# Attention and feed-forward layer: v loads behind the shift rows, the loop over sequences written out, constants filled as words, and another order of the copies of v

## What is computed

```python
xn  = layernorm(x)                                   # eps 1e-5
q, k, v = heads(xn @ Wq.T), heads(xn @ Wk.T), heads(xn @ Wv.T)
attend  = (abs(i - j) <= 128) | (i < 1) | (j < 1)    # a band, and token 0 to and from all
w   = softmax(where(attend, q @ k.T / sqrt(16), -inf))
x   = x + (w @ v) @ Wo.T
xn  = layernorm(x)
h   = bitlinear(xn, w_fc) + gate * (xn @ v2.T @ fast_b.T @ u.T)
out = x + bitlinear(relu(h) ** 2, w_proj)            # ternary weights with a scale
```

## Time and profile before

| | |
|---|---|
| median of 3 executions | 1406.53 us (1406.45 to 1410.13) |
| the profiled execution | 1413.2 us, span of its instructions 1410.8 us |
| mean granted TensorE clock | 0.936 of full speed |
| busy, of the span | PE 1223.1 us (87%), DVE 986.7 (70%), ACT 792.5 (56%), POOL 727.9 (52%) |
| DMA | 145.4 MB, queue of SP 37.8% of 16 engines' span |

### The profile page before, as it was taken

One profiled execution on the slowest core, in us unless ns is written; L12 is line 12 of the kernel. 1 busy time (PEld: TensorE's weight loads), 2 busy tenths in 40 slices (PEclk: granted clock), 3 DMA queues, 4 the chain that ended last, 5 costly groups with the idle time before them and its releaser, 6 DMA issues. The chain is left out here.

```text
span 1410.8 us, 31634 instructions
## 1 busy us (share of the span) xinstructions
PE 1223.1 (87%) x9122; PEld 807.0 (57%) x9122; DVE 986.7 (70%) x3217; ACT 792.5 (56%) x1315; POOL 727.9 (52%) x934
## 2 busy tenths in 40 slices
PE   4888885489998989889998998974699999999997
PEld 3777772044444444444444444433588888888886
DVE  5777762478787878678787787826477767777674
ACT  3555562067676767667676776762344545445454
POOL 1444443957676756667576675770143433433343
PEclk9999997589999999999999999995799999999999
DMA  2566754754246442455326543211311212122100
GB/s 86 194 221 221 234 193 117 124 119 110 69 105 150 115 118 72 107 119 133 97 79 136 120 105 99 60 56 45 120 46 46 90 45 89 45 61 72 45 31 30
DMA packets 141282, 145.43 MB, mean 103 GB/s; under 512 B 23085, under 2 KB 134721, under 8 KB 141121
## 3 DMA queue, kind: packets, MB, share of 16 engines
q1 hardware_dynamic: 141120, 143.55, 37.8%
HBM read 91.74 MB, written 50.95 MB: 101 GB/s over the span
## 5 line engine op out<-in xcount | busy, mean ns | idle before, releaser
L1124 DVE CUSTOM_DVE_ANT_0 a_masked<-a_turn,a_band 128x387 f32<-128x387 f32 (+1 forms) x1024 | 506.4, 537 | 128.4 <-PE a_turn L997 100.1
L1078 ACT ACTIVATE a_weights<-a_score 128x1024 f32<-128x1024 f32 x384 | 385.3, 1021 | 116.8 <-PE a_score L1017 116.3
L997 PE MATMUL a_turn<-a_k,a_q 96*128 96x387 bf16 (+1 forms) x1024 | 335.8, 339 | 23.2 <-DMA a_q<-q_parts 12.2
L1017 PE MATMUL a_score<-a_q,a_k 128*128 128x384 bf16 (+2 forms) x1408 | 282.3, 286 | 48.2 <-DMA a_q<-a_shift 47.8
L1381 POOL TENSOR_TENSOR f_square<-f_relu 128x512 f32<-128x512 f32 x128 | 150.5, 1179 | 296.4 <-ACT f_relu L1477 295.4
L894 POOL TENSOR_SCALAR_AFFINE_SELECT a_weights<-a_weights 128x1024 f32<-128x1024 f32 x256 | 275.8, 1090 | 53.2 <-ACT a_weights L1078 53.2
L997 PEld LDWEIGHTS a_turn<-a_k,a_q 96*128 96x128 bf16 x1024 | 96.8, 98 | 215.7 <-DVE a_max L1124 118.0
L1039 PE MATMUL a_sum<-a_weights,a_v 128*17 128x384 f32 (+2 forms) x2816 | 212.7, 400 | 2.3 <-POOL a_weights L894 2.2
L1017 PEld LDWEIGHTS a_score<-a_q,a_k 128*128 128x128 bf16 x1408 | 139.8, 101 | 110.5 <-issue 53.6
L1477 ACT ACTIVATE f_relu<-f_bank 128x512 f32<-128x512 f32 x128 | 76.5, 598 | 187.9 <-PE f_bank L207 184.7
L1509 DVE TENSOR_TENSOR f_square_lo<-f_square,f_square_hi 128x512 fp32r<-128x512 f32 x128 | 108.2, 856 | 88.8 <-POOL f_square L1381 88.8
(11 more groups left out here) (194 smaller groups left out, 2048.9 us busy)
## 6 DMA issues: line engine op xcount, KB each, us to landing
k_parts<-p_k_parts SPq DMA_DIRECT2D x96, 129.0 KB, 2.7
a_k<-k_parts SPq DMA_DIRECT2D x64, 193.5 KB, 3.7
a_k<-k_parts SPq DMA_DIRECT2D x192, 64.5 KB, 3.2
q_parts<-p_q_parts SPq DMA_DIRECT2D x96, 128.0 KB, 2.7
a_q<-q_parts SPq DMA_DIRECT2D x64, 192.0 KB, 3.3
a_q<-q_parts SPq DMA_DIRECT2D x192, 64.0 KB, 3.0
v_ones<-p_va SPq DMA_DIRECT2D x16, 544.0 KB, 3.4
p_x<-in_x SPq DMA_DIRECT2D x16, 512.0 KB, 5.1
```

The costliest lines, as they stand in the source:

```text
L997: pe.matmul(turn[TURN_OF_TILE[j] % TURN_BANKS][:, lo:hi], qw[ux.gpar][ux.hq][0:SLOT_ROWS, h, t * P:t * P + P], kt[ux.hq][0:SLOT_ROWS, h, s ...
L1017: ins = pe.matmul(score[c % 2][:, (n % 2) * GT + col * P:(n % 2) * GT + (col + m) * P], kt[us.hq][:, h, k0:k0 + P], qw[us.gpar][us.hq][:, ...
L1078: act.activation(pe_w[:, us.upar, c * CHUNK:(c + 1) * CHUNK], score[c % 2][:], ACT.Exp).then_inc(s_exp, 1)
L1124: dve.tensor_tensor_reduce(out=masked[:, ux.upar, h, t:t + hi - lo], in0=bank[:, lo:hi], in1=band[:, lo:hi], scale=1.0, scalar=NEG, op0=AL ...
```

## The change

- Projection: ACT makes the copies of v of the first two products ahead of the fourth middle part (`mid(2 * KT - 1)`) instead of behind it.
- `march`: the loop over sequences is a Python loop; all 64 units are written out, with constants in place of registers.
- SP in the attention: the load of v moves from `L_MAX` to `L_SHIFT`, one step later, and with `v0` behind the three shift rows of its step. The rows wait for a new semaphore of the zero fills (`s_zero`) in the first 8 units.
- The fills are made over fp32 words (a bitcast; one word of two bf16 ones for k), half the elements. POOL fills the eight q tiles first and then the k tiles 2 and 3; DVE fills the k tiles 0 and 1 ahead of its first unit. PE waits for each k tile by a semaphore of its own.
- The register waits (`Turn`) of POOL (`exp_turn`) and DVE (`tile_turn`) in the attention become waits for constants.

```diff
--- before.py
+++ after.py
@@ -47,6 +47,8 @@
 QSCALE = 1.0 / float(np.sqrt(HD))
 NEG = -3.0e38
 ROUND = 4
+
+TWO_ONES = float(np.array([0x3F803F80], np.uint32).view(np.float32)[0])
 DMA = 16
 
 
@@ -507,10 +509,11 @@
                     if u == 2 and (t := at(LN)):
                         norm.root(act, t)
                 if q:
-                    mid(2 * KT - 1)
                     if isinstance(q.g, int) and q.g == 0:
                         act.wait_ge(s_ones, 1)
                     for t in range(TB):
+                        if t == 2:
+                            mid(2 * KT - 1)
                         act.wait_ge(s_v, q.g * TB + t + 1)
                         act.activation(va[:, bass.ds(q.g * TB + t, 1), :].rearrange("p a (h e) -> p (a h) e", e=VW)
                                        [:, :, 0:HD],
@@ -651,9 +654,7 @@
             return Unit(b - 1, j + UPB)
         return at
 
-    for i in range(UPB):
-        body(step(0, i))
-    with eng.Fori(1, B) as b:
+    for b in range(B):
         for i in range(UPB):
             body(step(b, i))
     for i in range(lags):
@@ -771,7 +772,8 @@
         sum_bank = ctx.enter_context(nc.psum_tensor("a_sum", [P, GT], F32))
         turn = [ctx.enter_context(nc.psum_tensor(f"a_turn{i}", [P, GT], F32)) for i in range(TURN_BANKS)]
 
-        s_init, s_pool, s_ones = sem("init"), sem("pool_init"), sem("ones")
+        s_init, s_pool, s_zero = sem("init"), sem("pool_init"), sem("zero")
+        s_ones = [sem(f"ones{q}") for q in range(UPG)]
         s_load = [[sem(f"qk_in{g}{q}") for q in range(UPG)] for g in range(2)]
         s_v, s_v0 = [sem("v_in0"), sem("v_in1")], [sem(f"v0_in{q}") for q in range(UPG)]
         s_row = [sem("row0"), sem("row1")]
@@ -825,7 +827,16 @@
                         for n, part in enumerate(SINGLES[which]):
                             sp.dma_start(dst[(PARTS + n) * HD:(PARTS + n + 1) * HD], src[:, PLACE[which][part]]
                                          ).then_inc(landed, DMA)
-                if (u := at(L_MAX)) and u.hq == 0:
+                if u := at(L_SHIFT):
+                    if isinstance(u.n, int) and u.n < 2 * UPG:
+                        sp.wait_ge(s_zero, 2 * u.hq + 2)
+                    for part, ready in ((HIGH, s_high), (MID, s_mid), (LOW, s_low)):
+                        sp.wait_ge(ready, u.n + 1)
+                        row = qw[u.gpar][u.hq][SLOT_ROWS + part:SLOT_ROWS + part + 1, :, :]
+                        sp.dma_start(row.rearrange("s h (t q) -> s (h t) q", q=P),
+                                     shift[:, u.upar, part, :]).then_inc(s_row[u.upar], DMA)
+
+                if (u := at(L_SHIFT)) and u.hq == 0:
 
                     wait(sp, s_sum, (u.n - UPG * 2) + UPG)
                     lo, hi = window(u.gi)
@@ -838,15 +849,6 @@
                     cols = slice(u.hq * NQ * VW, (u.hq + 1) * NQ * VW)
                     sp.dma_start(v0[:, cols], va_dram[bass.ds(u.batch * T, 1), cols].to_broadcast((P, NQ * VW))
                                  ).then_inc(s_v0[u.hq], DMA)
-                if u := at(L_SHIFT):
-                    if isinstance(u.n, int) and u.n < 2 * UPG:
-                        sp.wait_ge(s_ones, u.hq + 1)
-                    for part, ready in ((HIGH, s_high), (MID, s_mid), (LOW, s_low)):
-                        sp.wait_ge(ready, u.n + 1)
-                        row = qw[u.gpar][u.hq][SLOT_ROWS + part:SLOT_ROWS + part + 1, :, :]
-                        sp.dma_start(row.rearrange("s h (t q) -> s (h t) q", q=P),
-                                     shift[:, u.upar, part, :]).then_inc(s_row[u.upar], DMA)
-
                 if (u := at(L_SHIFT)) and isinstance(u.n, int) and u.n == UNITS - 1:
                     ahead.load_weights(sp)
                 if (u := at(L_OUT)) and u.hq == UPG - 1:
@@ -879,16 +881,18 @@
                                pattern=[[0, NQ], [P, TB]], channel_multiplier=1).then_inc(s_pool, 1)
             pool.wait_ge(s_pool, 6)
             for q in range(UPG):
-                pool.memset(qw[0][q][SLOT_ROWS:P], 0.0)
-                pool.memset(qw[1][q][SLOT_ROWS:P], 0.0)
-                pool.memset(kt[q][SLOT_ROWS:P], 1.0).then_inc(s_ones, 1)
-                pool.wait_ge(s_ones, q + 1)
-            exp_turn = Turn(pool, s_exp, "exp_turn", CHUNKS // 2, CHUNKS // 2)
+                for g in range(2):
+                    pool.memset(qw[g][q][SLOT_ROWS:P].bitcast(F32), 0.0).then_inc(s_zero, 1)
+            for q in range(UPG // 2, UPG):
+                pool.memset(kt[q][SLOT_ROWS:P].bitcast(F32), TWO_ONES).then_inc(s_ones[q], 1)
+            pool.wait_ge(s_zero, 2 * UPG)
+            for q in range(UPG // 2, UPG):
+                pool.wait_ge(s_ones[q], 1)
 
             def cut(u, half, side):
 
                 if side == 0:
-                    exp_turn.wait(u.n * CHUNKS + (half + 1) * CHUNKS // 2)
+                    pool.wait_ge(s_exp, u.n * CHUNKS + (half + 1) * CHUNKS // 2)
                 first, sign = ((CUT_AHEAD, 1), (CUT_BEHIND, -1))[side]
                 blocks = pe_w[:, u.upar].rearrange("p (a c q) -> p a c q", a=2, q=P)[:, half, first::CUT_STEP, :]
                 pool.affine_select(out=blocks, in_=blocks, compare_op=ALU.is_ge, fill=0.0, base=0,
@@ -1006,7 +1010,7 @@
                     c = n // 2
                     if n == 0:
                         if isinstance(us.n, int) and us.n < UPG:
-                            pe.wait_ge(s_ones, us.n + 1)
+                            pe.wait_ge(s_ones[us.hq], 1)
                         pe.wait_ge(s_row[us.upar], (us.uhalf + 1) * DMA * SHIFT_ROWS)
                     if n % 2 == 0:
                         wait(pe, s_exp, us.n * CHUNKS + c - 1)
@@ -1101,8 +1105,9 @@
             dve.memset(score[1][:], 0.0).then_inc(s_init, 1)
             dve.memset(sum_bank[:], 0.0).then_inc(s_init, 1)
             dve.wait_ge(s_pool, 4)
+            for q in range(UPG // 2):
+                dve.memset(kt[q][SLOT_ROWS:P].bitcast(F32), TWO_ONES).then_inc(s_ones[q], 1)
             dve.wait_ge(s_pool, 6)
-            tile_turn = Turn(dve, s_tile, "tile_turn", 1)
 
             def body(at):
                 ux, um, uo = at(L_MAX), at(L_SHIFT), at(L_OUT)
@@ -1119,7 +1124,7 @@
                         bank, c = turn[TURN_OF_TILE[j] % TURN_BANKS], h * TB + t
                         if j == 0:
                             wait(dve, s_d0, ux.n - 1)
-                        tile_turn.wait(ux.n * TILES + j + 1)
+                        dve.wait_ge(s_tile, ux.n * TILES + j + 1)
 
                         dve.tensor_tensor_reduce(
                             out=masked[:, ux.upar, h, t:t + hi - lo], in0=bank[:, lo:hi],
```

## The result

| | before | after |
|---|---|---|
| median of the runs | 1406.49 us (1400.85 to 1410.13, 4 runs) | 1315.84 us (1313.05 to 1321.77, 4 runs) |
| the profiled execution | 1413.2 us, span 1410.8 | 1313.8 us, span 1312.1 |
| mean granted TensorE clock | 0.936 | 0.964 |

The changed kernel takes 0.936 of the time before (95% interval 0.932 to 0.941). The forecast was 1319 us, 1297 to 1347, and "faster" with 0.95: it held. The saving between the two profiled executions is 99 us where the sum of the forecast was 87. So the total came out, and the question is whether the parts did.

What follows compares the result with a forecast made beforehand. PE was taken as the bound, with its idle waits as the target. Savings of 20 + 16 + 33 + 13 + 5 = 87 us from the median of 1406.5 gave 1319 us, range 1297 to 1347.

Steps and rivals of the forecast that it cites:

- What bounds it: PE, busy 87% of the span, idles for the shift rows (47.8 us) and the projection's copies of v (24.3 us).
- Copies of v: Projection: two copies ahead of ACT's fourth middle part shorten PE's wait in each group; 20 us, ends 8 and 26.
- Fills: Attention's start: word fills by POOL and DVE let the first shift rows land sooner; 16 us, ends 14 and 18.
- rival D: Attention's start: fills cost by byte, so word fills are no shorter; 1322 us, chance 0.03.
- v behind the small transfers: Attention: without v ahead the shift rows land sooner, in ten waits of PE; 33 us, ends 15 and 43.
- Loop: Attention: writing the loop out removes the stop of all engines at two backward branches; 13 us, ends 9 and 14.
- Rival C: Attention: straight-line code can't be fetched as fast as five engines use it; slower, 1425 us, chance 0.03.
- Register waits: Attention: constant waits wake DVE sooner for a unit's first tile, 0.08 us in 60 units; 5 us, ends 0 and 15.
- A: Attention: rows stay late behind k, q and in four places the 127-row store; half of 33 us lost, 1336, chance 0.13.
- B: Projection: the gain is only 8 us because DVE or SP becomes its bound; 1331 us, chance 0.10.
- E: More comes free: PE's full clock earlier at the attention's start or no slow stretches in the projection; 1290, chance 0.06.

Runs made afterwards that it cites:

- n_act_dma: The changed kernel, but in the projection ACT instead of SP issues the store of v and the loads of x from the fifth group on; 0.924, 1304.0 us.
- a_fills_back: The changed kernel with the fills as before: bf16 elements, all twelve on POOL, in the old order; 0.947 of the time before, 1334.7 us.
- a_pool_only: The changed kernel, but POOL makes all the word fills and DVE none; 0.937 of the time before, 1318.3 us.
- n_store_late: The changed kernel, but SP waits for a finished group and stores it one step later, behind that step's loads and rows; 0.932, 1311.6 us.
- a_loop_back: The changed kernel with the loop over the last three sequences and the register waits of DVE and POOL back; 0.950, 1338.8 us.
- a_v_back: The changed kernel with the load of v again one step earlier and, like v0, ahead of the shift rows; 0.966, 1360.6 us.
- b_v_move: The kernel before with one edit alone: the load of v one step later and behind the shift rows, v0 behind it; 0.976, 1375.9 us.
- a_v_split: The changed kernel with v0 and only v's first 128 keys (136 KB) ahead of the rows, the rest behind; 0.935, 1319.9 us.
- a_v_back_128: a_v_back, but the first store of a sequence's first group writes 128 rows in place of 127; 0.953 of the time before, 1343.8 us.

## Why the prediction was right, and where not

**What bounds it.** Right. The two waits of PE that the argument began with were worth 76 of the 99 us (19.7 + 19.1 + 37.5). In the sum only a trifle was off: the low ends add up to 46, not 45.

**Copies of v.** 20 forecast, 19.7 measured at the last group. The period without PE's wait was forecast at 9.9 and is 9.75. The next bound was named (SP, 10.66 us a group with room of some 5 us) but its growth was mis-sized: I let SP fall behind 0.4 us a group because I kept a slow stretch of the clock every fourth group, as before. The slow stretches went with the waits, groups came at 9.75, SP fell behind by 1 us each, and the room was used up after the sixth. The sum was saved by a second error of the other sign, which is luck. I counted 1.5 us a group for the wait; the period fell by 1.7, and three of the four slow stretches went too. Without SP's bound, in n_act_dma, the last group stands 29.5 us sooner than before (214.15 to 184.61), beyond my upper end of 26; SP had taken back 10 of it.

**Fills.** The durations came out within 6%: POOL 0.90 us for 1024 words (0.87 forecast), 3.50 for 4128 (3.5), DVE 3.50 (3.7). The fills of after:

```profile
219.43 7.20 POOL L885 MEMSET a_q<- 32x1024 f32 x8
...
220.99 3.50 DVE L1109 MEMSET a_k<- 32x4128 f32 x1 [0.92 <-issue]
...
225.30 3.50 DVE L1109 MEMSET a_k<- 32x4128 f32 x1 [0.81 <-issue]
...
226.57 7.01 POOL L887 MEMSET a_k<- 32x4128 f32 x2
```

The Trainium skill's one cycle per element ("VectorE: DVE Perf Modes", section "Zero memsets can be issued as uint32"), at the 0.96 GHz of the same page, gives an estimate of 4.3 us for each of DVE's; the trace has 3.50, and the trace decides. On POOL an element costs the same at either width, 0.84 ns in a_fills_back (6.97 us for 8256) and 0.85 here (3.50 for 4128), and rival D is out. One step was wrong without harm: DVE's two fills don't fit into its gap. Each has 0.8 to 0.9 us of idle time ahead of it, and DVE's first tile starts 2.0 us later than in a_pool_only. That was "covered too", as the prediction said, because the rows are later still. What failed is the time of the rows: 16 forecast, 19.1 measured, outside the ends of 14 to 18. In n_store_late and a_loop_back, with the same start, the first step is 0.8 and 0.6 us longer, so that the gain lies 0.3 to 1.1 us beyond the upper end. I had the rows land at 269.3; they landed at 245.7, 266.8 on the old scale. I took the queue to be as late as before, less 2.0 us for v. From issue to landing the two rows took 5.7 us before, with v and `v0` ahead. In after the last of the three took 2.1 us, in n_store_late and a_loop_back 2.9, and in a_v_back, with v and `v0` ahead again, 5.0. So these two loads are worth 2 to 3 us here, about what I took for v. The rest is that the queue was less late already at the place where v had stood: the last load of q ahead of it took 5.0 us to land before, and the same load 3.3 in after. What shortened it, no run shows.

**v behind the small transfers.** The mechanism was right and is shown three ways: a_v_back, b_v_move, a_v_split. The idle time that goes was forecast at 22 of 27.8 us (its own caps, 2.0 and 2.9 us or the wait's length, add up to 20.8) and is 22.9. Mis-sized was the factor on it. I took 1.5 us lost per us idle where the row itself gave 6.1 for 3.7, which is 1.65, in order to allow for short waits. Measured is 39.2, less 1.7 for the register waits in these steps: 37.5 for 22.9, 1.64. A wait behind which the granted clock falls to its lower level costs its idle time and some 2.4 us more, as at unit 15 before; where the clock stays up, a wait costs little more than itself, 1.07 us per us in n_store_late. In after the clock stays at its upper level behind the wait of 1.17 us at unit 15:

```profile
387.50:394.40 6.90, 6.90 (x64) 3.38 (x64) 5.17 (x23) 5.20 (x8) 4.32 (x8) 1.00 0.72 171
```

So to keep the clock up takes away a surcharge at once, and a factor on the idle time hides that. In the kernel before, all seven waits of 3 us and more had a slow stretch and the three of 0.9 to 1.3 us none. In between, the length alone doesn't decide: behind a wait of 1.64 us in a_pool_only the mean clock fell to 0.75, behind one of 2.45 us in a_v_back it stayed at 1.00, and that wait's step is longer by 2.6 us, its own length and little more.

```profile
688.80:695.70 6.90, 6.90 (x50) 3.59 (x51) 4.27 (x17) 4.50 (x7) 3.23 (x7) 0.75 0.59 139
```

```profile
764.90:771.80 6.90, 6.90 (x65) 3.50 (x65) 5.47 (x23) 5.27 (x8) 3.33 (x8) 1.00 0.16 38
```

**Loop.** 13 forecast, 13.6 measured in the four steps; a_loop_back 11.9. Rival C, straight-line code that can't be fetched, is out: all 48 new units take the step of the first 16.

**Register waits.** 5 forecast; measured are 3.8 in the undisturbed steps, and 5.5 if the 17 others gained as much each. The 0.08 us a unit was a choice of mine: the rows gave 0.16 less 0.04, which is 0.12. DVE starts 0.03 to 0.04 us behind the product's end in after (0.16 before):

```profile
317.10 0.34 PE L1001 MATMUL a_turn<-a_k,a_q 96*128 96x387 bf16 x1
317.47 0.56 DVE L1129 CUSTOM_DVE_ANT_0 a_masked<-a_turn,a_band 128x387 f32<-128x387 f32 x1 [0.41 <-PE a_turn L1001]
```

**The other rivals.** A, that the rows stay late behind k, q and the store of 127 rows, didn't come, but its mechanism is real: a_v_back_128 shows that the store was worth 2.9 to 4.3 us of PE's wait at each of four places while v was ahead as well. Either of the two taken away was enough there: with v behind the rows the waits at these four units are 0.25 us or less in after, though its store has 127 rows. I had put A at 0.13 by the time it would give. By what causes the waits it deserved more. B came true in its mechanism (SP is the bound) and not in its size. E is part of the truth: the slow stretches of the projection went from four to one.

**Open.** 2.0 us less behind the last high row, where nothing is touched. Of the other kernels, whose code there is the same, some take up to 0.9 us less than the changed one and some up to 1.8 more, so that most of the 2.0 can be what executions differ by. That isn't shown.

## What to carry to other kernels

A small transfer that others wait for belongs ahead of the large ones on its queue, and behind nothing that its issuer has to wait for. When a wait of several microseconds goes, look at once at who was idle just as long beside it: here SP had 0.8 us a group to spare (10.66 of 11.5), and took back a third of what was won in the projection (10 of 29.5 us) until ACT issued two of its transfers. And price a wait of PE by its length and by the granted clock behind it, read from the window there: with a slow stretch a wait costs some 2.4 us more than its idle time, without one hardly more.

## What the hardware showed that I had not expected

- A store of 127 rows in place of 128, 127 KB, makes the transfers behind it late and SP's own issues longer (1.48 us in place of 0.60), and cost 21.5 us in four places of a kernel in which v stood ahead of those transfers too. Where v stood behind them, it cost next to nothing.
- An issue of SP costs 0.71 us for a store of 129 KB to the projection's arrays and 0.41 for one of 544 KB of v: it is not the bytes that set it. Three of the first merged into one took 1.07 us.
